# Attention and mixture of experts on one core: another order of work on all engines, VectorE's short chained steps set singly, the first expert buffers placed anew

## What is computed

```python
x = x + xattn(layernorm(x), ctx)      # softmax(q k^T / 16) v, context of 512 x 192
x = x + ffn(layernorm(x))
# ffn: probs = softmax(x Wr^T); top 2 of 8 experts, gates normalised;
#   h = gelu(x W1[e]^T + b1[e]);  y = h W2[e]^T + b2[e];  out += gate * y
```

## Time and profile before

| | us |
|---|---|
| median of 3 runs | 376.73 (376.52 to 377.44) |
| span of the profiled execution | 373.9 |
| PE busy in it | 336.9 |
| DVE, ACT, POOL busy | 272.9, 189.5, 122.7 |

### The profile page before, as it was taken

The page is one execution under the profiler, slowest core; times in us unless marked ns, Lnnn a source line. Parts: engine busy times, 40 slices in busy tenths (PEclk is TensorE's granted clock), DMA queues, the critical chain, the costliest instruction groups (busy, mean ns, idle before and its releaser), DMA issues.

```text
span 373.9 us, 8773 instructions
## 1 busy us (share of the span) xinstructions
PE 336.9 (90%) x2657; PEld 271.2 (73%) x2657; DVE 272.9 (73%) x753; ACT 189.5 (51%) x333; POOL 122.7 (33%) x124
## 2 busy tenths in 40 slices
PE   8998999789977849898699999999999999999980
PEld 4555765557645638787488888889898889988860
DVE  4259788987998699988777776756577776757760
ACT  2587798578577766171333334434454443445300
POOL 5017102382182173027623212233423132241322
PEclk9999999999989999999699999999999999999996
DMA  7977871465357326223425333434234333434312
GB/s 258 365 267 234 305 257 66 141 238 173 127 178 239 104 84 203 43 33 116 83 32 87 54 48 44 58 44 59 39 51 56 48 45 59 58 42 54 37 16 28
DMA packets 51112, 41.82 MB, mean 112 GB/s; under 512 B 28541, under 2 KB 46526, under 8 KB 50942
## 3 DMA queue, kind: packets, MB, share of 16 engines
q1 hardware_dynamic: 40798, 27.36, 26.0%
q0 software_dynamic: 7872, 11.77, 17.3%
q10 hardware_dynamic: 2400, 2.13, 1.7%
HBM read 22.28 MB, written 13.86 MB: 97 GB/s over the span
## 4 chain that ended last, share of the span: by engine, by line
PE 71%; DVE 16%; issue 5%; POOL 3%; ACT 1%; DMA 1%; POOLq 1%; DVEq 0%; SPq 0%; ACTq 0%
PE o_ps L781 26%; PE s_ps L763 15%; PE t_ps L763 13%; PE s_ps L637 3%; PE proj L624 3%; PE o_ps L656 3%; DVE w2l L1121 2%; DVE w1l L1121 2%; POOL rstd L503 2%; PE proj L603 2%; DVE negmax L1079 2%; PE o_ps L570 1%; PE proj L611 1%; POOL rows L516 1%; PE t_ps L647 1%
## 5 line engine op out<-in xcount | busy, mean ns | idle before, releaser
L548 POOL DMA_INDIRECT out<-y,xm x39 | 61.3, 1573 | 129.3 <-DVE y L1392 122.5
L969 ACT ACTIVATE g<-s_ps,b_sb,down 128x256 f32<-128x256 f32 (+1 forms) x100 | 45.4, 519 | 82.7 <-PE s_ps L763 72.2
L781 PE MATMUL o_ps<-w2h,gh 128*128 x312 | 85.0, 272 | 0.0
L781 PE MATMUL o_ps<-w2h,gl 128*128 x312 | 85.0, 272 | 0.0
L781 PE MATMUL o_ps<-w2l,gh 128*128 x312 | 85.0, 272 | 0.0
L1365 DVE TENSOR_SCALAR gh<-g,up 128x512 f16<-128x512 f32 x78 | 38.2, 489 | 36.5 <-ACT g L969 33.6
L969 ACT ACTIVATE g<-t_ps,b_sb,down 128x256 f32<-128x256 f32 (+1 forms) x92 | 42.3, 524 | 39.0 <-PE t_ps L763 38.6
L1367 DVE SCALAR_TENSOR_TENSOR gl<-g,up,gh 128x512 f16<-128x512 f32 x78 | 58.6, 752 | 2.8
L763 PE MATMUL s_ps<-xT,w1h 128*128 128x256 f16 (+1 forms) x400 | 52.3, 256 | 7.3 <-DVE w2l L1121 4.9
L763 PE MATMUL t_ps<-xT,w1h 128*128 128x256 f16 (+1 forms) x368 | 50.2, 261 | 0.8 <-issue 0.8
L516 POOL DMA_INDIRECT rows<-send,place x32 | 35.6, 1112 | 32.9 <-DVE place L1186 24.6
(11 more groups left out here) (231 smaller groups left out, 505.6 us busy)
## 6 DMA issues: line engine op xcount, KB each, us to landing
staged<-W2T SPq DMA_DIRECT2D x8, 1024.0 KB, 6.8
staged<-W1T SPq DMA_DIRECT2D x7, 1024.0 KB, 4.9
rows<-send POOLq DMA_DIRECT2D x8, 260.0 KB, 4.0
x_own<-x SPq DMA_DIRECT2D x2, 512.0 KB, 5.4
w2l<-W1T SPq DMA_DIRECT2D x1, 1024.0 KB, 10.3
out<-x_own ACTq DMA_DIRECT2D x2, 512.0 KB
b_sb<-b SPq DMA_DIRECT2D x1, 1024.0 KB, 5.5
out<-y,xm POOLq DMA_INDIRECT x39, 3.8
```

Source lines behind the costliest of these rows:

```text
L548: pool.indirect_dma_start(out=out, out_offset=bass.IndirectOffsetOnAxis(ap=xm[:, t % MB, r, META - 1:META].bitcast(I32), axis=0), in_=y2[: ...
L781: i = nc.tensor.matmul(y_ps[n % 2][:, 0:D], l[:, t % 2, m, r * P:(r + 1) * P], w[:, bass.ds(e, 1), m * D:(m + 1) * D].rearrange("p a n -> ...
L969: i = nc.scalar.activation(g[:, m, 0:width(t)], h_ps[group % 4][:, at:at + width(t)], ACT.Gelu, bias=b1_sb[:, bass.ds(e, 1), m:m + 1].rear ...
```

## The change

It does these things, and leaves the arithmetic as it is except where said:

- On DVE, `link` around most of attention's short steps becomes `mark(name, ins)`, which counts the end of the step, and `after(name)` ahead of the step that needs it. The steps become functions of their own and stand between other work. Several still follow each other directly.
- Fewer steps: eps is added on POOL, ahead of the power; the sums are read from PSUM with no copy (the biases' sums come once); `down` is made once for all units and `undo` in one step; the first expert's number and the gate are written straight to `send`; the two place steps are one.
- `first_table` moves from the end of batch 2 into batch 3, `early_table` from tile 0's end to batch 3 and to beside `split(0, ...)`.
- All four engines' orders in attention, and `projection_order` with them, are rewritten; in a middle batch `place` comes after both late residuals, and ahead of the last moments and the aggregate.
- Buffers: gh, b2_sb, y1 with y2 and late_hot, and g now cover staging 0, 1, 2, 3. PE waits for `low_ready` 13 before hidden(0), 14 before second(0), 15 before hidden(2), 16 before second(2). `low(14)` comes behind `ln2_apply(3)`, `low(15)` behind tile 1's splits.
- POOL's order stays.

```diff
-        g = sm("g", [P, MC, TR])
+        gh = sm("gh", [P, 2, MC, TR], F16)
         b2_sb = sm("b2_sb", [P, E, D])
-        gh = sm("gh", [P, 2, MC, TR], F16)
-        gl = sm("gl", [P, 2, MC, TR], F16)
-        xT = sm("xT", [P, XB, 2 * DC, TR], F16)
         y1 = sm("y1", [P, 2, D])
         y2 = sm("y2", [P, 2, 2, D])
-        late_hot, late_row, late_end = (sm(name, [P, LATE, SEG]) for name in ("late_hot", "late_row", "late_end"))
+        late_hot = sm("late_hot", [P, LATE, SEG])
+        unused = sm("unused", [P, DC * M - 6 * D - LATE * SEG])
+        g = sm("g", [P, MC, TR])
+        xT = sm("xT", [P, XB, 2 * DC, TR], F16)
+        gl = sm("gl", [P, 2, MC, TR], F16)
+        late_row, late_end = (sm(name, [P, LATE, SEG]) for name in ("late_row", "late_end"))
...
 
                 pool.wait_ge(var, b + 1)
+                roots[0] += 1
+                nc.gpsimd.tensor_scalar(vare[:, which, b * QT:(b + 1) * QT], mv[:, which, b * QT:(b + 1) * QT, 1],
+                                        EPS, None, ALU.add).then_inc(eps_added, 1)
+                pool.wait_ge(eps_added, roots[0])
                 nc.gpsimd.tensor_tensor(rstd[:, which, b * QT:(b + 1) * QT], vare[:, which, b * QT:(b + 1) * QT],
...
-                nc.tensor.matmul(bank[:, 0:4], ones32[:], sq[:, 2 * e:2 * e + 2, :].rearrange("p u c -> p (u c)"),
+                if e == 0:
+                    nc.tensor.matmul(bank[:, 2:2 + UNITS], ones32[:], sq[:, :, 1], start=True, stop=True)
+                nc.tensor.matmul(bank[:, 0:2], ones32[:], sq[:, 2 * e:2 * e + 2, 0],
                                  start=True, stop=True).then_inc(proj_full, 1)
...
+            for b in range(1, B - 1):
                 scores(b, 0)
                 scores(b, 1)
-                if b:
-                    add_all(2 * b)
-                    turn_normal(b - 1)
+                turn_normal(b - 1)
                 turn_probs(b, 0)
+                add_all(2 * b)
                 scores(b, 2)
-                if b:
-                    logits(b - 1)
+                logits(b - 1)
+                attend(b, 0)
                 turn_probs(b, 1)
                 scores(b, 3)
                 turn_probs(b, 2)
+                turn_x(b + 1)
                 attend(b, 1)
+                queries(b + 1)
                 turn_probs(b, 3)
                 attend(b, 2)
+                ranks(b - 1)
+                add_all(2 * b + 1)
                 attend(b, 3)
+                values(b + 1, range(0, 2))
+                values(b + 1, range(2, 4))
...
+            b = B - 1
+            scores(b, 0)
+            scores(b, 1)
+            turn_normal(b - 1)
+            turn_probs(b, 0)
+            add_all(2 * b)
+            scores(b, 2)
+            logits(b - 1)
+            turn_probs(b, 1)
+            attend(b, 0)
+            scores(b, 3)
+            turn_probs(b, 2)
+            attend(b, 1)
+            add_all(2 * b + 1)
+            ranks(b - 1)
+            turn_probs(b, 3)
+            attend(b, 2)
+            attend(b, 3)
...
-            pe.wait_ge(low_ready, 2 * FIRST_E)
+            pe.wait_ge(low_ready, 2 * FIRST_E - 1)
...
-                        pe.wait_ge(low_ready, UNITS)
+                        pe.wait_ge(low_ready, UNITS - 1)
...
+                if t == 0:
+                    pe.wait_ge(low_ready, 2 * FIRST_E)
+                if t == MINI:
+                    pe.wait_ge(low_ready, UNITS)
...
+            u = QT * b
+            soft(b, 0)
+            turned_rows("x2t", b - 1)
+            soft(b, 1)
+            square(u + 2)
+            take_turned(b, 0)
+            take_turned(b, 1)
+            take_logits(b - 1)
+            soft(b, 2)
+            high(u)
+            square(u + 3)
+            soft(b, 3)
+            take_turned(b, 2)
+            take_turned(b, 3)
+            high(u + 1)
+            high(u + 2)
+            high(u + 3)
+            store(b)
...
+            def mark(name, ins):
+
+                links[0] += 1
+                ins.then_inc(chain, 1)
+                at[name] = links[0]
+
+            def after(name):
+                dve.wait_ge(chain, at[name])
...
-                link(i)
-                tiles = slice(QT * b, QT * (b + 1))
-                nc.vector.tensor_scalar(vare[:, which, tiles], mv[:, which, tiles, 1], EPS, None, ALU.add).then_inc(done, 1)
+                i.then_inc(done, 1)
...
+            def route_less(b):
+                after("top")
+                mark("less_top", nc.vector.tensor_tensor(less_top[:], lg[:], wide(top[:]), ALU.subtract))
...
+            def place_sums(b):
+                after("place_of")
+                nc.vector.tensor_reduce(place[:, b, :, :], place_of[:], AX.X, ALU.max).then_inc(gate_ready, 1)
...
+            for b in range(1, B - 1):
                 u = QT * b
                 row_max(b, 0)
+                rows_high(b - 1)
                 row_max(b, 1)
+                low(u - 1, 0)
+                scale_bounds(2 * b)
+                ln1_moment(b + 1, 0)
+                scale_power(2 * b)
+                ln1_moment(b + 1, 1)
+                invert(b, 0)
+                ln1_moment(b + 1, 2)
+                scale_up(2 * b)
+                ln1_moment(b + 1, 3)
                 row_max(b, 2)
+                route_top(b - 1)
+                aggregate(0, b + 1, stats1_ready, ln_var)
+                rows_low(b - 1)
+                low(u - 1, 1)
+                ln1_apply(b + 1, 0)
+                route_less(b - 1)
+                ln1_apply(b + 1, 1)
+                route_first_at(b - 1)
+                ln1_apply(b + 1, 2)
+                ln1_apply(b + 1, 3)
+                route_first8(b - 1)
+                row_max(b, 3)
+                route_first_one(b - 1)
+                route_others(b - 1)
                 residual(b, 0)
+                ln2_moment(b, 0)
                 invert(b, 1)
+                low(u, 0)
+                route_gap(b - 1)
+                route_second_at(b - 1)
+                low(u, 1)
                 residual(b, 1)
+                route_second_rank(b - 1)
+                route_second8(b - 1)
+                ln2_moment(b, 1)
+                low(u + 1, 0)
+                route_second_one(b - 1)
+                route_chosen(b - 1)
+                gate_sum(b - 1)
+                low(u + 1, 1)
+                gate_first(b - 1)
+                scale_bounds(2 * b + 1)
                 invert(b, 2)
+                place_next(b - 1)
+                invert(b, 3)
                 residual(b, 2)
+                scale_power(2 * b + 1)
+                gate_second(b - 1)
+                ln2_moment(b, 2)
+                place_picks(b - 1)
                 residual(b, 3)
+                scale_up(2 * b + 1)
+                place_sums(b - 1)
+                ln2_moment(b, 3)
+                aggregate(1, b, stats2_ready, ln2_var)
+                low(u + 2, 0)
+                low(u + 2, 1)
+                ln2_apply(b)
...
+            b = B - 1
+            u = QT * b
+            first_have()
+            row_max(b, 0)
+            first_units()
+            rows_high(b - 1)
+            row_max(b, 1)
+            first_float()
+            low(u - 1, 0)
+            low(u - 1, 1)
+            first_scan()
+            first_begin()
+            rows_low(b - 1)
+            first_expert()
+            row_max(b, 2)
+            scale_bounds(2 * b)
+            first_hot()
+            scale_power(2 * b)
+            scale_up(2 * b)
+            route_top(b - 1)
+            invert(b, 0)
+            first_rows()
+            first_at_row()
+            route_less(b - 1)
+            route_first_at(b - 1)
+            route_first8(b - 1)
+            route_first_one(b - 1)
+            first_done()
+            route_others(b - 1)
+            route_gap(b - 1)
+            route_second_at(b - 1)
+            residual(b, 0)
+            route_second_rank(b - 1)
+            row_max(b, 3)
+            ln2_moment(b, 0)
+            route_second8(b - 1)
+            route_second_one(b - 1)
+            invert(b, 1)
+            route_chosen(b - 1)
+            residual(b, 1)
+            gate_sum(b - 1)
+            ln2_moment(b, 1)
+            gate_first(b - 1)
+            place_next(b - 1)
+            gate_second(b - 1)
+            scale_bounds(2 * b + 1)
+            place_picks(b - 1)
+            scale_power(2 * b + 1)
+            low(u, 0)
+            scale_up(2 * b + 1)
+            scales_down()
+            place_sums(b - 1)
+            early_have()
+            low(u, 1)
+            invert(b, 2)
+            scales_undo()
+            residual(b, 2)
+            early_units()
+            early_float()
+            ln2_moment(b, 2)
+            early_scan()
+            invert(b, 3)
+            early_begin()
+            residual(b, 3)
+            ln2_moment(b, 3)
+            low(u + 1, 0)
+            early_experts()
+            aggregate(1, b, stats2_ready, ln2_var)
+            early_hots()
```

(29 more changed lines are left out.)

566 lines of the change are left out of this document (319 added, 247 removed).

## The result

The changed kernel took 371.69 us (median of 4 runs, 370.53 to 372.23) beside 376.62 for the kernel before (376.09 to 377.44): ratio 0.9868, interval [0.9842, 0.9894]. It is faster, by 4.9 us; 9.6 were forecast. The time lies in the range (361.5 to 372.5), near its upper end.

What follows compares the result with a forecast made beforehand. PE was taken as busiest, waiting on chains through DVE and POOL, some 19 us within reach. 1.7 + 2.6 + 7.4 - 2.1 = 9.6 us, span 373.9 to 364.3, median 367.1; range 361.5 to 372.5.

Steps and rivals of the forecast that it cites:

- Batches 0 and 1: Start to `ln2_apply(1)`: fewer scales, one link less and an earlier `ln1_moments(1)` leave 1.7 us gained.
- Batch 2: From one `ln2_apply` to the next: 31.9 us instead of 34.5, 2.6 us saved.
- Batch 3: From `ln2_apply(2)` to hidden(0): PE waits for `low(12)`, no longer 13; 7.4 us gained.
- The first tiles: From hidden(0) to hidden(2): 21.4 us instead of 19.3, as PE arrives before the others; 2.1 us given back.
- rival (b): DVE's short steps don't get cheap, a step between long ones still pays 0.2 us: 371.5 us, chance 0.18.
- the forecast's own bounds: Steps at 0.07 or 0.21 us, eps step 0.2 or 1.0, root blocked or not: 363.5 to 370.5 us.
- Short steps: On DVE, a step standing singly between long ones costs some 0.1 us, a chained one 0.21.
- Eps on POOL: Adding eps on POOL saves DVE 0.2 us for two; DVE stands 1.1 us at `ln1_apply`.
- the rule weighed in the prediction: Two-SBUF-input VectorE and SBUF-reading GpSimd instructions contend, the later blocks fully; without it two batches are 1.6 us shorter together.
- Place, sends and root: End of a middle batch: POOL's four sends and root after place leave DVE idle 4.3 us ahead of every `ln2_apply`.
- (d): Slower: PE's instruction supply stops beside sends in the first tiles, 7.8 us per hole; 374.9 or 382.7 us, chance 0.09.
- (a): PE's hole at 177 us, beside hidden(4), goes away as tile and send fall together differently: 362.5 us, chance 0.15.

Runs made afterwards that it cites:

- A: Chip of the first group of four follow-up runs: the kernel before took 377.79 us there, the changed kernel run again 369.86 us, ratio 0.9807.
- C: Chip of the last group of four follow-up runs: the kernel before took 373.37 us there, the changed kernel run again 363.37 us, ratio 0.9734.
- chip B: Chip of the second group of four follow-up runs, all edits of the changed kernel: the kernel before took 373.05 us there.
- the third run: Changed kernel with POOL's ln2 root in batch 3 put ahead of all eight of batch 2's sends: 373.03 us, ratio 0.9879.

## Why the prediction was right in its sign and half wrong in its size

**The sum, step by step** (profiled executions, spans 373.9 and 370.4: 3.5 us of 9.6).

- *Batches 0 and 1*: 1.7 forecast, 0.26 measured at `ln2_apply(1)`. 0.75 of the miss is no work of the change: PE's first matmuls on loaded operands began at 7.07 instead of 6.32, and the first scores began at 18.82 instead of 18.07 (18.01 to 18.69 in three other runs of this start). The rest is put down to the eps step, treated below: with eps on DVE `ln2_apply(1)` came 1.3 earlier on A.
- *Batch 2*: 2.6 forecast, 3.2 measured (the period is 31.3 us, 31.9 forecast).
- *Batch 3*: 7.4 forecast, 6.4 measured (19.5 us from `ln2_apply(2)` to hidden(0), 18.5 forecast; PE waited 0.99 us for unit 15's square, 0.4 forecast, since the load took 6.9 us to reach ACT and not 5.8).
- *The first tiles*: 2.1 forecast to be given back, 5.8 measured. **This is the step that failed**, in three places. First, it was added up wrongly: its own terms, 1.3 for gelu(0) and 2.6 and 2.6 of waits, less 1.75 for hidden(0) and 1.09 for xT, come to 3.7 and not 2.1. Second, one wait was right (on C 2.55 us for the split behind `low(14)`, 2.6 forecast), one was shorter (1.61 for `ln2_apply(3)`, 2.6 forecast) and the one for gelu(0) did not come, but the text forgot what waits do to PE's clock: second(1) costs 2.4 us more. Third, hidden(0) was priced by a later single at 2.91. Its 4.66 before were at a low clock indeed (0.63 granted over them), but at 1.00 it still takes 3.7 in the profile after and 4.2 on C. The nearer row was in the trace of the kernel before, hidden(1), whose 48 matmuls took 4.0 us at a granted clock of 1.00 until second(0) began:

```profile
143.16 0.46 PE L763 MATMUL t_ps<-xT,w1h 128*128 128x128 f16 x4 [0.45 <-issue]
...
147.13 0.27 PE L781 MATMUL o_ps<-w2h,gh 128*128 x1
```

  Why they take 4 us there and 2.91 at 244 was not found out.
- *Beyond hidden(2)* the sum said nothing, and took it that what is won there lasts. 4.1 us were won at hidden(2), 5.3 at place of batch 3, 183.36 - 178.13 = 5.2 at SP's fetch of tile 5's rows, and 3.4 at hidden(5): the hole in hidden(4) took 1.8 more than before.

**The two holes.** Tile 5's rows reach PE 3.65 us after SP issues them (175.99 to 179.64 on C). By that hidden(5) could start at 187.0 before and at 181.8 after; it starts at 191.63 and 188.19. So by this estimate the hole in hidden(4) costs 4.6 and 6.4 us. Held against PE's own 26.4 us from hidden(2), it delays PE by 7.7 and 8.4; behind the late rows 3.1 of that were hidden before and 2.0 after. On C, with none in the changed kernel, the two kernels are 10.0 us apart; on A 7.9; in the first measurement 4.9. On C 7.4 of the 10.0 are those at SP's fetch (183.36 in the first measurement to 175.99). The other 2.6 stay open, as no trace of the kernel before on C or B was taken; that it loses its hole there is inferred from its time, 4.4 us below that on A.

**Luck.** The measured 371.69 us lie in the range only by the end that came from rival (b), which did not happen; the forecast's own bounds ended at 370.5. And the 10.0 us on C are near the 9.6 by accident: there too the first tiles took 25.1 us and not 21.4.

**Short steps.** Right: a step that stands singly costs 0.10 to the next start (57.90 to 58.00), a chained one 0.22 (as the last batch's routing, 154.22 to 154.44):

```profile
57.90 0.18 DVE L1238 TENSOR_TENSOR less_top<-lg,top 128x32 f32<-128x32 f32 x1
58.00 0.41 DVE L1104 TENSOR_SCALAR w2h<-w1h,mv,rstd 128x256 f32<-128x256 f32 x1
```

With the waits put back 7.4 of 10.0 us went (8.4 within chip B). That rules out rival (b) and makes this the part of the change that earns its time.

**Eps on POOL.** The two POOL steps beside `rows_low` and the half `low` behind it took 1.11 and 1.92 us, against 0.26 and 1.04 with nothing of that kind beside them, and DVE stood 0.93 at `ln1_apply` (1.1 forecast):

```profile
54.42 1.11 POOL L507 TENSOR_SCALAR vare<-mv 128x4 f32<-128x4 f32 x1 [8.15 <-DVE mv L1099]
55.61 1.92 POOL L510 TENSOR_TENSOR rstd<-vare,half 128x4 f32<-128x4 f32 x1
```

```profile
76.01 0.26 POOL L507 TENSOR_SCALAR vare<-mv 128x4 f32<-128x4 f32 x1
76.36 1.04 POOL L510 TENSOR_TENSOR rstd<-vare,half 128x4 f32<-128x4 f32 x1
```

Both steps are held up, the first until just behind the end of `rows_low` (54.25 + 1.19), the second until 0.9 after the half `low` (55.36 + 1.28). This agrees with the rule weighed in the prediction (the Trainium skill, page "SBUF — State Buffer", section "Who interferes with whom"). But the text said what DVE's idle costs and not that PE waits for it in the same place. The move back gained 3.5 us on A, more than twice the 1.6 named there, and 2.2 on C beside the late `low(14)`; on B, with two other edits, nothing clear of noise.

**Place, sends and root.** Half right. DVE idles 2.34 us for the root and 1.20 for ACT's `high` (4.3 forecast). With the root first, 3.9 us at `ln2_apply(2)` were 2.8 at PE's router and 0.9 at hidden(0). In the last batch PE waits 1.61 us for it on C.

**Rivals.** (d) came true in what it would look like, once more than before, and not at its price. The stops left hidden(1) when the sends did (the third run), but the new hole lay over waits that were there anyway. That it is PE's supply of instructions that stops is not shown. It had 0.09, with "those tiles ran beside sends before" against it; before, only hidden(0) did. (a), the hole gone, is what chip C shows for the changed kernel, at 363.37 us for the 362.5 it named; as a chance of this change it was wrongly set up, since the kernel before is 4.4 us faster there too.

## What to carry to other kernels

Follow every path to the stage that all engines share, before the sum is made. Here PE's logits and DVE's own list reached batch 3's routing within 0.03 us of each other: 5.5 us won on PE's path alone were worth 0.45, and a start of PE 7.1 us later cost nothing, as the waits behind it fell away. Before a small step is moved to an idle engine, look at what the busy one runs just then; the step that saved DVE 0.2 us for two cost the kernel 3.5 on one chip and 2.2 on another. And hold a gap marked "issue" against the same program on another chip before it is charged to the change.

## What the runs showed of the hardware that I had not expected

- The same program on chip A has two holes of PE ("issue" as the releaser) beside POOL's indirect DMAs and on chip C none, 369.86 against 363.37 us, at ratios of 0.9807 [0.9770, 0.9845] and 0.9734 [0.9701, 0.9767]. POOL's sends take 0.96 to 1.9 us each on both. The eight runs on B and C show no such hole, the four on A and the first measurement do. What differs between the chips isn't shown, nor what PE lacks in a hole.
- In such a hole ACT stops too: its second four gelus of tile 0 began 3.88 us late, with no engine of the core as the releaser (3.71 when the kernel ran again on A). Through ACT and the split the hole delays DVE as well, `ln2_apply(3)` to 142.16, 13.9 us behind hidden(0), where it was 12.1 behind it on C (139.15).

```profile
133.97 1.50 ACT L1036 ACTIVATE g<-s_ps,b_sb,down 128x128 f32<-128x128 f32 x4 [1.27 <-issue]
139.36 1.50 ACT L1036 ACTIVATE g<-s_ps,b_sb,down 128x128 f32<-128x128 f32 x4 [3.88 <-remote]
```

- A wait of PE can cost more than its length: 4.1 us idle in a stretch of 5.2 were followed by 5.1 us at a granted clock of 0.53, another 2.4 us.
